# Loading half the row blocks at twice the width in the second and third pass of a two-layer graph kernel

## The reference, cut to what matters

```
def _lap_mul(A, x):
    d = 1.0 / jnp.sqrt(jnp.sum(A, axis=-1))
    return d[:, None] * (A @ (d[:, None] * x))

# layer 0 (adj is 4096 x 4096 float32, x is 4096 x 128)
h = relu(layernorm(x))
z = leaky_relu(_lap_mul(adj, h) @ W1 + b1)          # first pass over adj
S = exp(-sqrt(pairwise_squared_distances(z)) / 2), only the 4 largest of each row kept
x = x + _lap_mul(S + adj, h) @ W2 + b2              # second pass over adj
# layer 1
h = relu(layernorm(x))
x = x + h @ W_self.T + (adj @ h) @ W_neigh.T + b    # third pass over adj
```

## Time and profile before

| | us |
|---|---|
| three runs | 1497.4, 1495.37, 1486.2 |
| median | 1495.37 |
| profiled execution, its time | 1488.5 |
| its span in the trace | 1486.7 |
| PE busy | 1065.4 (72%) |
| DVE busy | 871.5 (59%) |
| ACT busy | 406.9 (27%) |
| POOL busy | 475.3 (32%) |
| mean granted clock of PE | 0.867 of 2.4 GHz |

### The profile page before, as it was taken

How to read it: one execution, slowest core, us unless ns; L and a number is a source line. 1 busy time by engine, 2 the same in 40 slices (tenths; PEclk the granted TensorE clock), 3 DMA queues, 4 the chain that set the end, 5 groups by cost and what they waited for, 6 DMA issues and landing times.

```text
span 1486.7 us, 12333 instructions
## 1 busy us (share of the span) xinstructions
PE 1065.4 (72%) x3170; PEld 609.4 (41%) x3170; DVE 871.5 (59%) x888; ACT 406.9 (27%) x997; POOL 475.3 (32%) x572
## 2 busy tenths in 40 slices
PE   0315556689787887899994778878697637878687
PEld 0202222334343366677773333433243314545444
DVE  1514553566655557799997737666465625545453
ACT  0534433554221054455552000000000102222131
POOL 1101111114121023344443175445344014535354
PEclk9956667899899988999997898989799877989899
DMA  9999999999999497443346899999999499999992
GB/s 191 189 222 198 224 211 195 202 223 196 183 198 220 101 217 169 158 168 144 134 174 148 194 237 241 211 248 236 201 253 219 102 206 218 261 230 226 210 232 52
DMA packets 254467, 291.36 MB, mean 196 GB/s; under 512 B 21600, under 2 KB 231520, under 8 KB 254432
## 3 DMA queue, kind: packets, MB, share of 16 engines
q1 hardware_dynamic: 161888, 162.49, 47.5%
q10 hardware_dynamic: 72576, 67.12, 20.1%
q0 software_dynamic: 19968, 61.36, 18.7%
HBM read 251.07 MB, written 39.85 MB: 196 GB/s over the span
## 4 chain that ended last, share of the span: by engine, by line
DMA 19%; DVE 14%; PE 11%; issue 8%; SPq 7%; ACTq 6%; POOL 4%; ACT 2%; DVEq 1%; POOLq 0%
DMA araw<-in_adj_dram 17%; SPq L358 7%; ACTq L358 4%; DVE tr L844 4%; POOL sq_rows L594 2%; PE ps L1313 2%; DVE m L987 2%; ACTq L774 2%; DVE i L989 2%; DVE bmax L974 2%; DMA t_st<-keys_scratch,block_row 2%; DVE out_t L1054 1%; PE ps L1257 1%; PE ps L1275 1%; PE ps L1260 1%
## 5 line engine op out<-in xcount | busy, mean ns | idle before, releaser
L844 DVE STREAM_TRANSPOSE tr<-araw 128x2048 f32<-128x2048 f32 (+3 forms) x244 | 441.6, 1839 | 363.4 <-DMA araw<-in_adj_dram 259.3
L1275 PE MATMUL ps<-tr,ys 128*128 128x512 f32 x512 | 256.2, 658 | 93.6 <-DVE tr L844 55.6
L1164 PE MATMUL ps<-tr,ys 128*128 128x512 f32 x448 | 236.7, 678 | 103.3 <-DVE tr L844 103.3
L358 POOL DMA_DIRECT2D araw<-in_adj_dram x120 | 77.7, 652 | 402.0 <-DVE tr L844 233.7
L1275 PEld LDWEIGHTS ps<-tr,ys 128*128 128x128 f32 x512 | 105.7, 213 | 230.0 <-issue 173.5
L1164 PEld LDWEIGHTS ps<-tr,ys 128*128 128x128 f32 x448 | 93.4, 218 | 221.4 <-issue 144.3
L705 ACT ACTIVATE araw<-ps,nsq 128x1024 f32<-128x1024 f32 x128 | 142.7, 1117 | 128.7 <-PE ps L1260 97.9
L594 POOL TENSOR_TENSOR sq_rows<-tr,zt_lo 128x2048 fp32r<-128x2048 f32 x28 | 126.8, 4536 | 158.2 <-ACT zt_lo L780 158.2
L553 POOL DMA_INDIRECT zt_lo<-neighbour_table,idx_st x128 | 129.8, 1014 | 46.0 <-issue 41.1
L627 ACT ACTIVATE ps<-araw 128x256 f32<-128x256 f32 x304 | 111.1, 366 | 61.4 <-DMA araw<-in_adj_dram 60.9
L1257 PE MATMUL ps<-sq_rows,pick 128*128 128x512 f32 x256 | 103.9, 406 | 26.2 <-POOL zs_lo L470 17.9
(11 more groups left out here) (138 smaller groups left out, 1043.8 us busy)
## 6 DMA issues: line engine op xcount, KB each, us to landing
araw<-in_adj_dram SPq DMA_DIRECT2D x200, 512.0 KB
araw<-in_adj_dram ACTq DMA_DIRECT2D x120, 512.0 KB
araw<-in_adj_dram POOLq DMA_DIRECT2D x64, 512.0 KB, 16.0
keys_scratch<-araw SPq DMA_DIRECT2D x64, 512.0 KB, 3.6
xs<-in_x_dram SPq DMA_DIRECT2D x8, 512.0 KB, 7.7
araw<-in_adj_dram POOLq DMA_DIRECT2D x16, 256.0 KB, 8.9
araw<-in_adj_dram SPq DMA_DIRECT2D x16, 256.0 KB
araw<-in_adj_dram POOLq DMA_DIRECT2D x8, 448.0 KB, 10.6
```

What stands on the lines that cost most here:

```text
L358: eng.dma_start(araw[R * q:R * q + R, slot, :, at:at + cols], src).then_inc(landed[slot], DMA)
L844: return v.transpose(out.rearrange("p t (m s) -> p t m s", s=R), src)
L1164: pe.matmul(acc[bank], ys[:, c * GROUPS + first + i], ring1[:, (k + i) % RING1], start=start and i == 0, stop=stop and i == tiles - 1).the ...
L1275: ins = pe.matmul(acc[bank], src[:, j * U + i], tr[:, j % TSLOTS, i], start=j == 0 and i == 0, stop=j == GROUPS - 1 and i == U - 1)
```

## The change

A slot of `araw` now takes half the row blocks (8 of 16) and 512 columns of each quarter. The bytes of a slot and of a transfer are as before; the contiguous pieces in memory are 2 KB. Loads n = 0 and 1 are the upper and lower half of the row blocks for the first 512 columns (units 0 to 3), loads 2 and 3 the same for units 4 to 7. A unit needs both halves. DVE transposes it with two instructions of 128x1024. It takes load n's part of all four units before it goes to load n+1, so that 16 transposes make a group (`STEPS`), and a slot of `araw` is free after four. `t_ready` counts these halves, and PE and ACT wait with `unit_ready` for a unit's second half. The wait for a free `tr` slot stands before the first half of each unit. DVE's `finish_second_c` and `finish_third` stand behind the second halves of units 0 to 3, `finish_second_a` behind the first halves of units 4 to 7, `finish_second_b` behind the last. In ACT's third pass load 2 moves from behind `split_high(g, 6)` to ahead of `store`. In the third pass's group 0 both halves of a unit are transposed together, in the old order of units.

```
+HALF_COLS = 2 * CHUNK_COLS
+HALF_UNITS = GROUPS // 2
+STEPS = 2 * GROUPS
...
+    adj_h = adj.rearrange("(h m g r) (q w c) -> q r g w h m c", h=2, m=QD * U // 2, g=GROUPS, q=QD, w=2)
...
-        def load_chunk(eng, g2, g, c, quarters):
-
-            taken = CHUNKS + c + 1 if isinstance(g2, int) and g2 == GROUPS + 1 else (c + 1) * CHUNK_UNITS
-            eng.wait_ge(t_ready, g2 * GROUPS + (UNITS1 + taken - GROUPS))
-            load(eng, c, g, c * CHUNK_COLS, CHUNK_COLS, quarters)
+        def load_half(eng, n, g, quarters):
+
+            w, h = divmod(n, 2)
+            for q in quarters:
...
+                eng.dma_start(ahalf[n][R * q:R * q + R], src).then_inc(a_in[n], DMA)
+
+        def load_after(eng, g2, g, n, quarters):
+
+            if isinstance(g2, int) and g2 == 1 and n == 0:
+                taken = HALF_UNITS * 2
+            elif isinstance(g2, int) and g2 == GROUPS + 1:
+                taken = (3 + n // 2) * HALF_UNITS
+            else:
+                taken = (n + 1) * HALF_UNITS
+            eng.wait_ge(t_ready, g2 * STEPS + (UNITS1 + taken - STEPS))
+            load_half(eng, n, g, quarters)
+
+        def unit_ready(g, j):
+
+            if isinstance(g, int) and g == 0 and j < HALF_UNITS:
+                return UNITS1 + (3, 4, 7, 8)[j]
+            return g * STEPS + (UNITS1 + j // HALF_UNITS * GROUPS + HALF_UNITS + j % HALF_UNITS + 1)
...
                 split_high(g, 4)
                 if loads:
                     load_third(g, 1)
+                    load_third(g, 2)
                 store(g - 1, 1 - i)
                 split_high(g, 6)
                 if loads:
-                    load_third(g, 2)
                     load_third(g, 3)
...
             def group_second(g, i, prev, before, first=0):
-                for j in range(first, GROUPS):
-                    product_unit(g, j, 0, USED1)
-                    if j == 3 and before is not None:
+                for n in range(SLOTS):
+                    half_landed(n, g, 0)
+                    for j in range(max(first, n // 2 * HALF_UNITS), (n // 2 + 1) * HALF_UNITS):
+                        if n % 2 == 0:
+                            slot_free(g, USED1, j)
+                        half_unit(n, j, j)
+                    if n == 1 and before is not None:
                         finish_second_c(before)
-                    if prev is not None:
-                        if j == 6:
-                            finish_second_a(prev, 1 - i)
-                        if j == 7:
-                            finish_second_b(prev)
+                    if n == 2 and prev is not None:
+                        finish_second_a(prev, 1 - i)
+                    if n == 3 and prev is not None:
+                        finish_second_b(prev)
...
             def group_third(g, i, prev):
-                for j in range(GROUPS):
-                    after_split = j % 2 == 0 and not (isinstance(g, int) and j < TSLOTS)
-                    product_unit(g, j, GROUPS, USED1 + UNITS, slot_split=split_units(g, j) - 1 if after_split else None)
-                    if j == 2 and isinstance(g, int):
+                for n in range(SLOTS):
+                    half_landed(n, g, GROUPS)
+                    for j in range(n // 2 * HALF_UNITS, (n // 2 + 1) * HALF_UNITS):
+                        after_split = j % 2 == 0 and not (isinstance(g, int) and j < TSLOTS)
+                        if n % 2 == 0:
+                            slot_free(g, USED1 + UNITS, j, split_units(g, j) - 1 if after_split else None)
+                        half_unit(n, j, j)
+                    if n == 1 and isinstance(g, int):
                         finish_second_c(GROUPS - 1)
-                    if j == 3:
+                    if n == 1:
                         finish_third(prev, 1 - i)
...
             for place, j in enumerate(EVENS_FIRST):
-                product_unit(0, j, GROUPS, USED1 + UNITS, place)
+                slot_free(0, USED1 + UNITS, place)
+                for h in range(2):
+                    n = j // HALF_UNITS * 2 + h
+                    half_landed(n, 0, GROUPS)
+                    half_unit(n, j, place)
```

More of the change, by code:

```diff
@@ L114, in gnn_kernel @@
         stats4 = sb("stats4", [P, U, 6])
+        ahalf = [araw[:, n].rearrange("p m c -> p (m c)").rearrange("p (m c) -> p m c", c=HALF_COLS) for n in range(SLOTS)]
         xs_g = xs[:].rearrange("p (u g) f -> p g u f", g=GROUPS)
@@ L421, in _ @@
                 keys_store(1 + n)
-                load(sp, n, 0, n * CHUNK_COLS, CHUNK_COLS, ALL)
+                load_half(sp, n, 0, ALL)
             with sp.Fori(1 + SLOTS // 2, TILES // 2) as pair:
@@ L441, in load_group @@
                 for c in range(CHUNKS):
-                    load_chunk(sp, g2, g, c, LOW)
-            with sp.Fori(1, GROUPS + 1) as g2:
+                    load_after(sp, g2, g, c, LOW)
+            load_group(1)
+            with sp.Fori(2, GROUPS + 1) as g2:
                 load_group(g2)
@@ L734, in load_high @@
                 for c in chunks:
[L735 removed]
+                    load_after(act, g2, g, c, HIGH)
             def finish_second(g, last_chunk=True):
@@ L1011, in _, with half_landed, half_unit, slot_free @@
             v.tensor_scalar(vals_f, vals_f, 1e-10, None, ALU.add).then_inc(s_arg, 1)
[L1013 to L1018, removed]
+            def half_landed(n, g, base_group):
+                v.wait_ge(a_in[n], (g + base_group + 1) * PER_LOAD + loads_in[n])
+            def half_unit(n, j, place):
+                w, h = divmod(n, 2)
+                src = ahalf[n][:, :, (j - w * HALF_UNITS) * UNIT_COLS:(j - w * HALF_UNITS + 1) * UNIT_COLS]
+                dst = tr[:, place % TSLOTS, :, h * (GI // 2):(h + 1) * (GI // 2)]
+                v.transpose(dst.rearrange("p t (m s) -> p t m s", s=R),
+                            src.rearrange("p m (t s) -> p t m s", s=R)).then_inc(t_ready, 1)
+            def slot_free(g, base_unit, place, slot_split=None):
                 if slot_split is not None:
@@ L1022, in product_unit @@
                     v.wait_ge(t_used, g * GROUPS + (base_unit + place - TSLOTS + 1))
-                transposed(tr[:, place % TSLOTS], c, half * UNIT_COLS, U).then_inc(t_ready, 1)
-            for j in range(2):
-                product_unit(0, j, 0, USED1)
+            for n in range(2):
+                half_landed(n, 0, 0)
+                for j in range(2):
+                    if n == 0:
+                        slot_free(0, USED1, j)
+                    half_unit(n, j, j)
             v.wait_ge(s_exp, 1)
@@ L1298, in group_second @@
                         pe.wait_ge(y_ready, GROUPS + j + 1)
-                    unit(g, j, i, UNITS1, ys)
+                    unit(g, j, i, 0, ys)
                     if j == 0 and before is not None:
@@ L1327, in group_third @@
                     else:
-                        unit(g, j, i, UNITS1 + UNITS, hs)
+                        unit(g, j, i, GROUPS, hs)
                     if prev is not None and j == 0:
@@ L1342, in _ @@
             for place, j in enumerate(EVENS_FIRST):
-                pe.wait_ge(t_ready, UNITS1 + UNITS + place + 1)
+                pe.wait_ge(t_ready, UNITS1 + GROUPS * STEPS + 2 * (place + 1))
                 for i in range(U):
```

17 lines of the change are left out of this document (11 added, 6 removed).

## The result

The changed kernel takes 1568.6 us (median of five runs, 1563.7 to 1579.0). The kernel before took 1497.4 beside it. The ratio is 1.050, with a 95% interval of 1.045 to 1.055. The change makes the kernel slower by 5%. The profiled execution took 1579.0, the longest of the five, with a span of 1577.2.

What follows compares the result with a forecast made beforehand. Memory was taken to bound both passes before the change, PE and DVE in turn after it; +2.5, +27, -14, +81 and +12 gave +108, 1488.5 to 1597 profiled, 1600 as median, range 1540 to 1650.

Steps and rivals of the forecast that it cites:

- start, group 0: Start of the second pass: ACT's half of load 0 waits for units 0 to 3, group 1 comes later, +2.5 us.
- second pass, seven groups: Second pass: six groups at 46.5 us and the last at 43, 322 us for 295, +27.
- between the passes: From second to third pass: with slots loaded ahead, 53 us in place of 67.6, -14.
- third pass, six groups: Third pass: six groups at 51 us each against 37.5, 306 us for 225, +81.
- The signs named ahead: Both passes: groups of 46 to 47 and 48 to 54 us, DMA share 0.6 to 0.85, DVE and PE waiting on each other.
- PE busy on the ring: Second pass before the change: PE had ready units in `tr` to work on while `finish_second_a` ran for 7.9 us.
- The four turns of the working: Second-pass group: units 0 to 3, idle PE with `finish_second_a`, units 4 to 7, idle PE again; 46.5 us together.
- "light" case: Both passes: PE stays warm and stores cost 1.78 us, groups of 43.1 and 45.5 us, 1542 up to 1565; chance 0.12.
- upper row: Third-pass group: four stores' issues at 7.83 us give 53.5 us, at 1.78 give 48.3; 51 taken, nearer the former.
- Faster pieces don't help: Second pass: a 46.5 us group asks memory for 202 GB/s, less than it gives now, so shorter packets gain nothing.
- The heavy rival: Third pass: issues of 3 us on ACT delay unit 6's copy and a load, 58 us a group, 1640; chance 0.12.
- The first rival: Both passes: PE's and DVE's turns overlap, memory decides with shorter packets, 4 to 5 us less a group, 1440; chance 0.09.

Runs made afterwards that it cites:

- order_1k: The changed kernel with its transfers cut back to 1 KB pieces (all row blocks, 256 columns a load), order of halves kept: 1672.9 us, ratio 1.130.
- order_1k_act: The changed kernel with 1 KB pieces and, in ACT's third pass, the copy of unit 6 moved ahead of the issues: 1613.6 us, ratio 1.086.
- pieces_2k: The kernel before, in its own order of units, with the changed kernel's transfers of 2 KB pieces: 1364.5 us, ratio 0.911.
- load2_back: The changed kernel with ACT's load 2 of the third pass back behind the copy of unit 6: 1576.1 us, ratio 1.058.
- pairwise: The changed kernel, transfers kept, with both halves of a unit transposed one behind the other and ACT's loads 2 and 3 together: 1441.6 us, ratio 0.967.
- pair_late: The changed kernel with both halves of a unit transposed together, `finish_second_a` behind unit 7 and ACT's four second-pass loads ahead of its wait: 1377.2 us, ratio 0.931.
- staggered: pair_late with the halves transposed one unit apart, so that the first half's slot comes free two transposes sooner: 1405.2 us, ratio 0.949.

## Why the prediction was right

The sign was right, and the time fell inside the range, 31 us below the predicted 1600. Part of that distance is the spread of executions: I put the median 7 us above the profiled execution, so that 1597 should have given 1604 and not 1600. Measured, the median lies 10 us below it (1568.6 for 1579.0). The steps, on the profiled executions (1488.5 and 1579.0, a difference of 90.5 where 108 was summed):

| step | predicted | measured | from |
|---|---|---|---|
| ahead of the second pass | 0 | -6.1 | PE's first unit at 825.81, now 819.74 |
| start, group 0 | +2.5 | +4.2 | 38.7 us to group 1, now 43.0 |
| second pass, seven groups | +27 | +34.7 | 295.1, now 329.8 |
| between the passes | -14 | -15.5 | 67.6, now 52.1 (1192.49 to 1244.60) |
| third pass, six groups | +81 | +62.7 | 225.1, now 287.8 |
| last group | +12 | +10.5 | 34.3, now 44.9 |

The 6 us ahead of the second pass, which the change doesn't touch, are chance: order_1k and order_1k_act have the same instructions up to there and came to it 17 us apart. The sum came within 18 us because its errors have both signs: the second pass 8 too low and the third 18 too high.

*The order of halves sets the pace.* Shown from two sides: order_1k and the changed kernel have the same group of the second pass to 0.1 us, with pieces of half the length, and pieces_2k, which lacks the order, does a group in 33.4 us. The signs named ahead held in kind, DVE's waits name PE and PE's name DVE, but the DMA share in 900:1000, 0.87, lies above the 0.85, and the groups of 47.7 and 47.9 just outside 46 to 47 and 48 to 54. I had read the earlier trace rows with "PE busy on the ring"; it had one unit, as shown above, which changes nothing in the sum.

*The second pass, 46.5 predicted and 47.7 measured.* The four turns of the working came out as follows. Units 0 to 3 took 17.9 us (predicted 18.0), the idle stretch with `finish_second_a` 10.4 (10.3), units 4 to 7 17.0 (15.7), the second idle stretch 2.5 (2.5). The whole error is in the units behind the long idle stretch: I took one cold unit at 5.2 and three warm ones, as behind the 6.50 us of the earlier trace rows. The granted clock, the third column from the end in these stretches of the changed kernel, shows more:

```profile
1032.00:1037.00 5.00, 5.00 (x6) 2.11 (x7) 3.48 (x5) 0.35 (x1) 0.00 (x0) 0.50 0.52 155
1037.00:1049.00 12.00, 11.90 (x27) 4.90 (x25) 3.80 (x4) 1.30 (x4) 8.24 (x10) 0.96 0.76 184
```

For 5 us behind the idle stretch the clock is 0.50 of 2.4 GHz, that is 1.2 GHz, then 0.96. Six times 1.2 us is 7 of the 8 us that the second pass came out longer. The "light" case, in which PE stays warm (43.1 us), is real too: it is the first half of load2_back's second pass, at 44.6.

*The third pass, 51 predicted and 47.9 measured.* The step that was mis-sized is the stores. I put ACT's four issues between 1.78 and 7.83 us and leaned to the upper row "because that one is of this pass". Measured: 2.47. The lower bound of the working was 48.3. PE starts unit 6 right behind unit 5 (in the chain, 2.76 at 1325.79 behind 3.43 at 1322.36), so the copy of unit 6 wasn't late, and the sign that POOL and PE wait for ACT behind the stores didn't come. Six groups at 3.1 us less are the 18 us by which the third pass was over-charged. The earlier trace rows was the wrong neighbour since those stores stood behind full queues of 1 KB pieces.

*Between the passes, -14 predicted and -15.5 measured.* ACT's eight issues, 24.26 us in the earlier trace rows, took 11.77. ACT and PE in order of time:

```profile
1216.53 11.77 ACTq L394 DMA_DIRECT2D araw<-in_adj_dram  x8
...
1244.60 0.77 PE L1359 MATMUL ps<-sq_rows,zt_hi 128*128 128x512 f32 x1 [20.36 <-POOL sq_rows L621]
```

*Packets, 101 to 125 ns predicted.* 112 in pieces_2k, where the queues are as full as in the earlier trace rows. In the changed kernel the same ratio gives 0.386 x 1600 / 4644 = 133 ns, above the range, at a share of 0.87. What a packet waits for there is not shown.

*"Faster pieces don't help".* Right for the second pass alone. In the third they spare 13 us a group (60.9 against 47.9) by the issues on ACT, and the sum had no term for it: the short issues were taken from a lower demand on memory, and order_1k shows that with a lower demand still (130 GB/s) the issues are long if the pieces are 1 KB. The heavy rival had half of the mechanism, the late copy and not the late load, and a good price (58 us a group, 1640; order_1k gave 60.9 and 1673) for a kernel with 1 KB pieces.

*The first rival, memory decides, 1440.* Its condition, overlapping turns, is met in pairwise, pair_late and pieces_2k, and its price was far too small: I let a group fall by 4 to 5 us and held the rest to be PE's and ACT's. pair_late saves 8.8 us of the second pass's group and 5.6 of the third's.

The Trainium skill ("DMA: Bandwidth & Descriptors", section "Why small descriptors are slow (HBM only)") gives by its 3 cycles a packet an estimated 4% for the step from 1 to 2 KB; here the packets gave 20% (141 to 112 ns) and the rate 25% (230 to 287 GB/s), so the measurement decides against its figure. (The rival at that price, put at 1465, is 1472 with the 7 us that the 1440 beside it has.)

## What to carry to other kernels

A wider transfer and the order in which its parts are consumed are two edits. Here the pieces alone gave -9% and the order alone +13% (+9% with ACT's copy ahead of the issues), and the two together hid a kernel that is 7% faster than before. When a buffer slot holds half of what a unit needs, finish units one by one as soon as both halves are there, and put other work of that engine (here 7.9 us of sums) where a complete unit lies ready for the next engine. Before taking an issue's duration from a row, look at what stood in its queue: the length of the pieces queued changes how long the engine that issues is held, and with it everything behind it.

## What the runs showed of the hardware

- In the second pass (900:1000), with a DMA share of 0.96 to 1.03, pieces of 1 KB moved 230 GB/s, of 2 KB 287 and of 4 KB 294. A packet took 70.4 ns with 1 KB, 112 with 2 KB and 200 with 4 KB. A full share is not a rate: staggered moved 242 GB/s in 1230:1300 at 0.98, pair_late 269 in 1220:1290 at 1.01.
- The engine that issues is held by what its queue already holds, and that goes by the number of pieces. ACT's eight loads of 512 KB at the start of the third pass took 24.26 us with 1 KB pieces, 11.77 and 10.86 with 2 KB (the changed kernel, pieces_2k) and 3.70 with 4 KB. Issue by issue: with 1 KB the second one already took 3.4 us; with 2 KB the first five took 0.3 to 0.5 each and the last three 2.0 to 3.4; with 4 KB none took over 0.46.

```profile
1117.40 10.86 ACTq L393 DMA_DIRECT2D araw<-in_adj_dram  x8
```

```profile
1114.47 3.70 ACTq L392 DMA_DIRECT2D araw<-in_adj_dram  x8
```

- An issue behind such a queue is held too, whatever its own pieces. The same four stores of 64 KB took 7.83 to 10.11 us behind loads of 1 KB pieces and 2.47 behind 2 KB. A full memory isn't the reason: the 10.11 us fell at a DMA share of 0.87 to 1.00, and four stores in pieces_2k took 2.03 and 3.32 us at 1.07 and more.
- A merged row of issues can hold waits for semaphores as well. The eight of pieces_2k at the start of the second pass stand in one row of 24.18 us, and their own durations add up to 5.5.
- The same idle stretches of 2.46 and 10.4 us gave units of 5.40 and four units of 17.0 us in the changed kernel, with a granted clock of 0.50 (1.2 GHz) behind both, and 3.70 and 15.69 us in the first groups of load2_back, where the clock stayed at 1.00 (2.4 GHz) behind the short one and was back sooner behind the long one. PE's clock took either course with the same work around it.
